# Softmax denominators from summed key blocks, with the sum made on GpSimd, in a fused macaron block on one Trainium2 core

## The chip, the cores and the metric

The kernel runs on one core of one Trainium2 chip. The metric is the device time of one execution in microseconds (us); lower is better. The engines are TensorE (PE, with its weight loads as PEld), VectorE (DVE), ScalarE (ACT), GpSimd (POOL) and SyncE (SP, which issues most of the DMAs here). Each works through its own queue in program order; semaphores order them among each other.

## The reference

For 16 batches of 512 tokens with 128 features, everything in fp32:

```python
x = x + 0.5 * ffn(layernorm(x))     # 128x128 weight rounded to int4 steps, bias, rank-16 LoRA
x = x + attention(layernorm(x))
x = x + 0.5 * ffn(layernorm(x))

# attention: 16 heads, head size 64, keys and values from a latent of 32 per token
q = einsum('bld,dhk->blhk', x, Wq);  latent = einsum('bld,dc->blc', x, Wkv_down)
k = einsum('blc,chk->blhk', latent, Wk_up);  v = einsum('blc,chk->blhk', latent, Wv_up)
p = softmax(causal(q @ k.T / 8))     # 512 x 512 per head
y = einsum('bhqk,bkhd->bqhd', p, v);  out = einsum('bqhd,hdo->bqo', y, Wout)
```

## The kernel before, in words

The key and value projections are folded into the query and output weights, so that scores and weighted sums are taken against the 32-wide latents. There are H = 16 heads in G = 4 groups of HG = 4, and four key blocks of P = 128 keys.

A *round* `t` handles several batches at once: attention of batch t (`attend`), the row maxima of batch t+1 (`top`), the first feed-forward, queries and keys of batch t+2 (`prep`, "front units") and projection and second feed-forward of batch t-1 (`end`, "tail units"). Rounds go from -2 to 16, so rounds 1 to 13 hold all four kinds of work. A round has 16 steps; step s = 4g + j is group g and key block j. By causality block j only matters for queries from 128j on, so a step has 512 - 128j query columns per head: 512, 384, 256, 128.

The order in a step is written out by hand for each engine:

- TensorE, `score(s, e)`: scores with keys on the partitions, up to 512 columns in one of two PSUM banks. One call fills a bank: one head in blocks 0 and 1, two heads (256 columns each) in block 2, four heads (128 each) in block 3, with one matmul per head. A bank may be overwritten when ACT has read it (`exp_done`, two units back).
- ACT, `exp(s, e)`: one exponential per bank, into `probs`, four buffers of [128, 4 heads, 512], one per step in turn. Each is free again when `pv_done` says that TensorE has finished with it.
- POOL: one `affine_select` per step zeroes the upper triangle of the diagonal 128x128 blocks of the four heads, and signals `p_ready`.
- TensorE, two steps later (`LAG` = 2), between its second and third score calls: `weigh_latents` multiplies the probabilities of step s-2 with the latents (four matmuls, one per head, each with 32 output partitions of one bank, `y_bank`); `weigh_ones` multiplies the same probabilities with ones, which adds up each query's denominator. `group_ones` puts the four groups' sums on different partitions, and `den_bank` accumulates over all 16 steps.
- Maximum units, 41 a round: one or two matmuls into one of three ring banks and a VectorE reduction each (`max_unit`). The table `A_AT` lists for each step where among the scores they stand (slots 0 to 5).
- ACT copies `y_bank` to `y_sb` after each group and `den_bank` to `den` in step 2 of the next round. VectorE inverts `den` (steps 2, 3) and spreads it over the heads with shuffles (steps 4, 5). POOL multiplies (`scale_y(0..3)`, four times 512 elements) to `y_norm`, in steps 5 and 6; TensorE's `project_out` in step 7 needs all four.
- POOL also does small chains for the layer norms (`scale_and_bias`, with a power of -0.5; `first_rstd` in step 14) and adds the bias in two places (`xb`, `x2b`). VectorE normalises the next-but-two batch in step 15 (line 898: four `tensor_scalar` of 128 columns, SBUF to SBUF), and TensorE's first front unit in step 0 transposes the result.

## Time and profile before

| | |
|---|---|
| median of 3 runs | 1002.56 us (999.51 to 1003.19) |
| the profiled execution's own time | 1000.99 us |
| its span in the profile | 999.3 us |
| a full round (from one copy of `den` to the next) | 56.1 us |
| the last round with attention | 40.4 us |
| TensorE / VectorE / ACT / GpSimd busy in the span | 94% / 68% / 54% / 36% |
| granted TensorE clock, mean | 0.974 |

Times are those of one profiled execution. A busy TensorE is not one at its peak: matmuls overlap, and their ends are modelled, so the distance from one start to the next tells what an instruction costs.

### The profile page before, as it was taken

Reading aid. Unit: us, or ns where it says so; the run is one execution under the profiler, and the core shown is the slowest. Engines: PE = TensorE matmul, PEld = TensorE weight load, DVE = VectorE, ACT = ScalarE, POOL = GpSimd, SP = SyncE. Lnnn points to the kernel's source line nnn. Section 1 sums busy time; section 2 is a strip of 40 time slices with the busy share of each in tenths; the row PEclk is TensorE's granted clock in tenths of the full one; section 3 lists DMA queues with packets and bytes.
Section 4 is the critical chain, followed back from the end, with each engine's and each line's share of the span. In section 5 each row is a group of like instructions: output and inputs, shape, how many; then the busy total and the mean of one; then the engine's idle time right before and its main releaser. Section 6 shows DMA issues by size and latency. Waiting matters only on the chain. (4 is left out here: it accounts for less than half of the span.)

```text
span 999.3 us, 20244 instructions
## 1 busy us (share of the span) xinstructions
PE 936.8 (94%) x7518; PEld 579.5 (58%) x7518; DVE 677.7 (68%) x1526; ACT 536.5 (54%) x1065; POOL 364.4 (36%) x551
## 2 busy tenths in 40 slices
PE   4678999999999999999999999999999999999873
PEld 3345556566565656566565666566565666555433
DVE  4468577778767677678767677678767677576311
ACT  3242655556655555556656555556656555545550
POOL 4101234353433424253433425253533525233333
PEclk9968999999999999999999999999999999999995
DMA  3436251433425141433425141433425241420000
GB/s 81 96 81 139 52 114 45 96 95 76 115 64 125 41 104 47 101 89 76 115 65 126 43 102 47 103 88 76 114 65 125 48 99 34 108 62 12 13 22 11
DMA packets 77538, 77.81 MB, mean 78 GB/s; under 512 B 9392, under 2 KB 51136, under 8 KB 77440
## 3 DMA queue, kind: packets, MB, share of 16 engines
q1 hardware_dynamic: 75296, 74.76, 31.7%
q10 hardware_dynamic: 2144, 1.75, 0.7%
q8 instruction: 60, 0.98, 0.4%
q14 instruction: 38, 0.31, 0.1%
HBM read 9.90 MB, written 8.39 MB: 18 GB/s over the span
## 5 line engine op out<-in xcount | busy, mean ns | idle before, releaser
L470 ACT ACTIVATE probs<-bank 128x512 f32<-128x512 f32 (+1 forms) x704 | 376.3, 559 | 309.9 <-PE bank L591 307.2
L421 POOL TENSOR_SCALAR_AFFINE_SELECT probs<-probs 128x512 f32<-128x512 f32 x256 | 162.8, 637 | 531.9 <-ACT probs L470 530.6
L848 DVE TENSOR_REDUCE maxima<-bank 128x1 f32<-128x512 f32 (+1 forms) x384 | 255.9, 681 | 124.6 <-PE bank L649 124.3
L591 PE MATMUL bank<-q_stack,keys 123*128 123x512 f32 (+3 forms) x1024 | 326.0, 384 | 4.8 <-ACT probs L470 4.5
L649 PE MATMUL bank<-keys,q_stack 122*128 122x512 f32 (+3 forms) x1024 | 256.4, 333 | 7.0 <-DMA q_stack<-q_low 2.8
L649 PEld LDWEIGHTS bank<-keys,q_stack 122*128 122x128 f32 x1024 | 177.4, 193 | 97.8 <-issue 46.2
L591 PEld LDWEIGHTS bank<-q_stack,keys 123*128 123x128 f32 x1024 | 167.8, 190 | 101.9 <-issue 52.0
L848 DVE TENSOR_REDUCE block_max<-bank 128x4 f32<-128x512 f32 x256 | 174.3, 681 | 34.3 <-PE bank L649 34.1
L605 PE MATMUL bank<-probs,lat 128*32 128x512 f32 (+3 forms) x2048 | 190.9, 444 | 1.0 <-ACT y_sb L477 0.6
L616 PE MATMUL bank<-probs,group_ones 128*32 128x512 f32 (+3 forms) x2048 | 185.2, 433 | 0.6 <-ACT den L519 0.5
L616 PEld LDWEIGHTS bank<-probs,group_ones 128*32 128x32 f32 x2048 | 63.9, 110 | 78.9 <-issue 53.8
L397 POOL TENSOR_TENSOR y_norm<-y_sb,y_norm 128x512 f32<-128x512 f32 x64 | 80.5, 1281 | 6.6 <-DVE y_norm L866 6.6
L674 PE MATMUL bank<-xn_t,w_query 128*128 128x512 f32 x128 | 71.4, 645 | 4.7 <-DVE q_low L914 2.9
L499 ACT ACTIVATE q_high<-bank 128x512 fp32r<-128x512 f32 x64 | 38.4, 600 | 65.0 <-PE bank L674 64.8
L698 PE MATMUL bank<-w_out,y_norm 128*128 128x128 f32 x512 | 62.6, 283 | 10.4 <-POOL y_norm L397 10.4
L605 PEld LDWEIGHTS bank<-probs,lat 128*32 128x32 f32 x2048 | 40.6, 108 | 53.7 <-issue 37.8
L698 PEld LDWEIGHTS bank<-w_out,y_norm 128*128 128x128 f32 x512 | 62.2, 199 | 11.9 <-issue 11.3
L861 DVE RECIPROCAL den_inv<-den 128x128 f32<-128x128 f32 x64 | 55.8, 916 | 12.6 <-ACT den L519 12.6
L880 DVE TENSOR_TENSOR x<-bank,x_back 128x512 f32<-128x512 f32 x16 | 11.1, 692 | 56.5 <-PE bank L698 56.5
L914 DVE TENSOR_TENSOR q_low<-bank,q_high 128x512 fp32r<-128x512 f32 x64 | 43.6, 681 | 6.9 <-ACT q_high L499 6.9
L866 DVE STREAM_SHUFFLE y_norm<-den_inv 128x512 f32<-128x512 f32 x64 | 46.0, 749 | 0.0
L477 ACT ACTIVATE y_sb<-bank 128x512 f32<-128x512 f32 x64 | 38.0, 593 | 4.7 <-POOL y_norm L397 2.8
(106 smaller groups left out, 632.4 us busy)
## 6 DMA issues: line engine op xcount, KB each, us to landing
q_stack<-q_high SPq DMA_DIRECT2D x256, 128.0 KB, 2.4
q_stack<-q_low SPq DMA_DIRECT2D x128, 128.0 KB, 2.5
out_dram<-x SPq DMA_DIRECT2D x32, 256.0 KB, 2.4
x_in<-in_L_attn_x_bld_dram SPq DMA_DIRECT2D x16, 256.0 KB, 3.3
x_back<-out_dram SPq DMA_DIRECT2D x16, 256.0 KB, 3.1
keys<-keys_staged SPq DMA_DIRECT2D x15, 192.0 KB, 2.5
keys<-keys_staged SPq DMA_DIRECT2D x30, 96.0 KB, 2.3
lat<-lat_staged SPq DMA_DIRECT2D x16, 64.0 KB, 1.9
```

Of the source, the lines that this page charges most:

```text
L397: nc.gpsimd.tensor_tensor(y_norm[:, g, :], y_sb[:, g, :], y_norm[:, g, :], ALU.mult).then_inc(y_normed, 1)
L421: nc.gpsimd.affine_select(out=diag, in_=diag, compare_op=ALU.is_ge, fill=0.0, base=0, pattern=[[0, HG], [1, n]], channel_multiplier=-1).th ...
L470: nc.scalar.activation(probs[s % BUFS][:, e:e + heads, 0:n], scores[u % 2][:, 0:heads * n].rearrange("p (e q) -> p e q", e=heads), ACT.Exp ...
L591: last = nc.tensor.matmul(scores[u % 2][:, i * n:(i + 1) * n], keys[par][:, PLAIN_BLOCK[j], :], q_stack[par][:, g * HG + e + i, j * P:L], ...
L605: last = nc.tensor.matmul(y_bank[e * LD:(e + 1) * LD, j * P:L], lat[(par + off) % 2][:, j, :], probs[s % BUFS][:, e, 0:L - P * j], start=( ...
L616: last = nc.tensor.matmul(den_bank[e * LD:(e + 1) * LD, j * P:L], group_ones[:, g, :], probs[s % BUFS][:, e, 0:L - P * j], start=(s == 0), ...
L649: last = nc.tensor.matmul(bank[:, col:col + n], q_stack[1 - par][0:KC, half * HALF + h, j * P:(j + 1) * P], keys[1 - par][0:KC, blocks, :] ...
L674: last = nc.tensor.matmul(bank[:], w, xn_t[:], start=True, stop=True)
L698: last = nc.tensor.matmul(aux[:, i * D:(i + 1) * D], y_norm[:, g, i * P:(i + 1) * P], w_out[:, g, :], start=(g == 0), stop=(g == G - 1))
L848: nc.vector.tensor_reduce(out, seg, AX.X, ALU.max).then_inc(a_free, 1)
L861: nc.vector.reciprocal(den_inv[:, part], den[:, part]).then_inc(den_made, 1)
L866: nc.vector.stream_shuffle(y_norm[:, g, :], den_inv[:], [g] * LD).then_inc(den_made, 1)
```

## The change

1. The denominators take fewer matmuls. GpSimd adds the probabilities of key blocks 1 and 2 onto those of block 0 (`add_probs`), in place, for the queries that they share (384 and 256 columns of each head). Each addition is made in two parts of two heads: 768 elements per partition twice and 512 twice in a group. `weigh_ones` is now called once per group, in step 4g+5, and takes block 0 with the sum, and block 3.
2. The additions stand in POOL's queue in steps 4g+2 and 4g+3, one part in front of the step's select and one behind. The first waits until the latents of step 4g are weighed, since it overwrites their input. The pieces that POOL has in the queue besides are moved: `scale_y` to steps 4, 5, 5, 6; `scale_and_bias` one step earlier, behind the select.
3. The probabilities' buffers change: two for block 0 (`first_probs`) and one each for blocks 1, 2, 3 (`later_probs`). `pv_done` is signalled after the latents; `added` and `den_done` are new.
4. `weigh_latents` moves behind the step's third score slot in steps with j = 3.
5. `score` issues one matmul over all heads that share a bank (2 x 256 or 4 x 128 columns) in place of one per head.
6. `A_AT` is another table; the number of units is the same.

```diff
-A_AT = [[], [0, 1, 1], [0, 2, 3], [], [2, 3, 3, 5], [0, 5], [1, 4], [2, 2], [0, 3, 3, 5], [0, 1, 4], [0, 2], [0, 1, 1, 4, 5], [0, 1, 2, 3], [0, 0, 1, 3], [1, 2], [4]]
+A_AT = [[], [1, 1, 2], [0, 2], [3, 5], [0, 2, 5], [0, 1, 1, 5], [0], [1], [3], [0, 1, 4, 5], [0, 1, 1, 2, 4], [4, 5, 5], [0, 2, 3], [0, 1, 4, 5], [0, 0, 2, 3], [5]]
...
+WEIGH = [[2], [2], [2], [2]]
+WEIGH_SLOT = [1, 1, 1, 3]
+WEIGH_ONES = [[], [2], [], []]
+PARTS = 2
+ADD_AT = [(1, 0, 2, 0), (1, 1, 2, 1), (2, 0, 3, 0), (2, 1, 3, 1)]
+SCALE_AT = [4, 5, 5, 6]
...
-BUFS = 4
+ADDED = [1, 2]
+DEN_PARTS = [j for j in range(TT) if j not in ADDED]
...
-        probs = [sb(f"probs{i}", [P, HG, L]) for i in range(BUFS)]
+        first_probs = [sb(f"first_probs{i}", [P, HG, L]) for i in range(2)]
+        later_probs = [sb(f"later_probs{j}", [P, HG, L - P * j]) for j in range(1, TT)]
...
+                def add_probs(off, g, j, part):
+
+                    turn = PARTS * (g * len(ADDED) + ADDED.index(j)) + part
+                    wait_batch(pool, pv_done, t, off, STEPS, g * TT + 1)
+                    wait_batch(pool, p_ready, t, off, STEPS, g * TT + j + 1)
+                    if j != ADDED[0]:
+                        wait_batch(pool, added, t, off, PARTS * G * len(ADDED), turn - PARTS + 1)
+                    heads = slice(part * HG // PARTS, (part + 1) * HG // PARTS)
+                    total = first_probs[g % 2][:, heads, j * P:L]
+                    nc.gpsimd.tensor_tensor(total, total, later_probs[j - 1][:, heads], ALU.add).then_inc(added, 1)
+
+                def adds(s, behind):
+
+                    for j, part, step, at in ADD_AT:
+                        if at == behind and (s - step) % TT == 0:
+                            if s >= step and attend:
+                                add_probs(0, (s - step) // TT, j, part)
+                            if s < step and end:
+                                add_probs(-1, (s - step + STEPS) // TT, j, part)
...
-                    if prep and s == FRONT_AT[1] + 2:
+                    for g in range(G):
+                        if end and s == SCALE_AT[g]:
+                            scale_y(g)
+                    adds(s, 0)
+                    if attend:
...
+                    if prep and s == FRONT_AT[1] + 1:
                         wait_batch(pool, f_normed, t, 1, 2, 2)
                         scale_and_bias(f_moments, 2, 2, f_mv[:, 1], f_var[:, 1], f_rstd[:, 1], f_shift,
                                        f_pool, 4, f_rstd_made)
...
+                    if end and s == TAIL_AT[0] + 1:
                         wait_batch(pool, t_normed, t, -2, 1, 1)
                         scale_and_bias(t_moments, 1, -1, t_mv, t_var[:], t_rstd[:], t_shift, t_pool, 3, t_rstd_made)
...
+                    adds(s, 1)
...
                     if e == 0:
-                        wait_batch(act, pv_done, t, 0, STEPS, s - BUFS + 1)
+                        wait_batch(act, pv_done, t, 0, STEPS, s - TT + 1)
+                        if j in ADDED:
+                            wait_batch(act, added, t, 0, PARTS * G * len(ADDED),
+                                       PARTS * ((g - 1) * len(ADDED) + ADDED.index(j) + 1))
+                        else:
+                            wait_batch(act, den_done, t, 0, G, g if j else g - 1)
...
-                    for i in range(heads):
-                        last = nc.tensor.matmul(scores[u % 2][:, i * n:(i + 1) * n], keys[par][:, PLAIN_BLOCK[j], :],
-                                                q_stack[par][:, g * HG + e + i, j * P:L], start=True, stop=True)
-                    last.then_inc(s_full, 1)
+                    first = g * HG + e
+                    nc.tensor.matmul(scores[u % 2][:, 0:heads * n], keys[par][:, PLAIN_BLOCK[j], :],
+                                     q_stack[par][:, first:first + heads, j * P:L], start=True, stop=True).then_inc(s_full, 1)
...
+                def weigh_ones(off, g):
+
+                    if g == 0:
                         wait_batch(pe, den_free, t, off, 1, 0)
-                    for e in range(HG):
...
-                    last.then_inc(pv_done, 1)
+                    for j in DEN_PARTS:
+                        if j == 0:
+                            wait_batch(pe, added, t, off, PARTS * G * len(ADDED), PARTS * (g + 1) * len(ADDED))
+                        else:
+                            wait_batch(pe, p_ready, t, off, STEPS, g * TT + j + 1)
+                        for e in range(HG):
+                            last = nc.tensor.matmul(den_bank[e * LD:(e + 1) * LD, j * P:L], group_ones[:, g, :],
+                                                    probs_of(g * TT + j)[:, e, 0:L - P * j],
+                                                    start=(g == 0 and j == 0),
+                                                    stop=(g == G - 1 and j == DEN_PARTS[-1]))
+                    last.then_inc(den_done, 1)
```

## Rows read from the trace of the kernel before

**Rows 1.** The page: span; busy us (share) and instructions by engine.

```profile
span 999.3 us, 20244 instructions
...
PE 936.8 (94%) x7518; PEld 579.5 (58%) x7518; DVE 677.7 (68%) x1526; ACT 536.5 (54%) x1065; POOL 364.4 (36%) x551
...
```

**Rows 2.** Waits: who waited for whom, us in total, times, longest.

```profile
...
POOL probs L421 <- ACT probs L470: 530.6, 176, 8.0
...
PEld bank L591 <- ACT probs L470: 46.3, 153, 0.9
...
```

**Rows 3.** Windows: length, busy us (instructions) by engine, granted clock, DMA.

```profile
...
372.70:428.80 56.10, 55.97 (x468) 34.75 (x464) 41.54 (x95) 32.47 (x68) 22.26 (x33) 1.00 0.36 86
...
877.40:928.80 51.40, 49.71 (x432) 29.52 (x424) 32.29 (x65) 27.35 (x56) 18.03 (x26) 1.00 0.12 29
928.80:969.20 40.40, 36.82 (x353) 19.43 (x346) 8.74 (x22) 22.55 (x46) 17.00 (x24) 1.00 0.05 14
969.20:979.20 10.00, 0.00 (x0) 0.00 (x0) 6.04 (x12) 0.60 (x2) 4.94 (x4) 0.60 0.00 0
...
```

**Rows 4.** Timeline, TensorE, a steady round: start us, us, what.

```profile
...
429.41 1.07 PE L616 MATMUL bank<-probs,group_ones 128*32 128x512 f32 x8
430.41 0.51 PE L649 MATMUL bank<-keys,q_stack 122*128 122x256 f32 x2
...
431.23 0.56 PE L591 MATMUL bank<-q_stack,keys 123*128 123x128 f32 x4
431.72 0.85 PE L605 MATMUL bank<-probs,lat 128*32 128x384 f32 x8
432.39 0.83 PE L616 MATMUL bank<-probs,group_ones 128*32 128x384 f32 x8
...
433.81 0.64 PE L605 MATMUL bank<-probs,lat 128*32 128x256 f32 x8
434.27 0.61 PE L616 MATMUL bank<-probs,group_ones 128*32 128x256 f32 x8
...
435.15 0.45 PE L591 MATMUL bank<-q_stack,keys 123*128 123x512 f32 x1
435.43 0.62 PE L649 MATMUL bank<-keys,q_stack 122*128 122x512 f32 x3
...
438.13 0.43 PE L605 MATMUL bank<-probs,lat 128*32 128x128 f32 x8
...
445.98 3.73 PE L698 MATMUL bank<-w_out,y_norm 128*128 128x128 f32 x32
...
454.50 0.43 PE L605 MATMUL bank<-probs,lat 128*32 128x128 f32 x8
...
473.04 1.04 PE L616 MATMUL bank<-probs,group_ones 128*32 128x512 f32 x8
...
481.93 0.43 PE L605 MATMUL bank<-probs,lat 128*32 128x128 f32 x8
...
```

**Rows 5.** Groups by form, POOL: busy us, mean ns of one, idle before.

```profile
...
L397 POOL TENSOR_TENSOR y_norm<-y_sb,y_norm 128x512 f32<-128x512 f32 x64 | 80.5, 1281 | 6.6 <-DVE y_norm L866 6.6
...
L385 POOL TENSOR_TENSOR t_shift<-t_shift,t_rstd 128x4 f32<-128x4 f32 x16 | 3.3, 204 | 1.3
...
```

**Rows 6.** Timeline of POOL in the same round.

```profile
...
432.57 0.23 POOL L380 TENSOR_SCALAR f_var<-f_mv 128x4 f32<-128x4 f32 x1
...
434.46 0.64 POOL L421 TENSOR_SCALAR_AFFINE_SELECT probs<-probs 128x512 f32<-128x512 f32 x1
...
438.47 2.51 POOL L397 TENSOR_TENSOR y_norm<-y_sb,y_norm 128x512 f32<-128x512 f32 x2
...
```

**Rows 7.** Timeline of POOL and DVE around line 898, twice.

```profile
...
44.45 1.26 POOL L425 TENSOR_TENSOR xb<-x_in,half_bias 128x512 f32<-128x512 f32 x1
44.52 2.05 DVE L898 TENSOR_SCALAR xn<-x_in,f_mv,f_rstd 128x128 f32<-128x128 f32 x4 [0.87 <-POOL f_rstd L391]
...
478.88 1.11 DVE L898 TENSOR_SCALAR xn<-x_in,f_mv,f_rstd 128x128 f32<-128x128 f32 x4
...
```

More of the change, by code:

```diff
@@ L213, in macaron_block @@
         pv_done = sem("pv_done")
-        y_full = sem("y_full")
+        added = sem("added")
+        den_done = sem("den_done")
         y_free = sem("y_free")
@@ L233, in wait_batch_alone, with probs_of @@
             eng.sem_inc(waits_passed, 1)
+        def probs_of(s):
+            return later_probs[s % TT - 1] if s % TT else first_probs[s // TT % 2]
         def stages(t):
@@ L474, in read_y @@
                 def read_y(off, g):
-                    wait_batch(act, y_full, t, off, G, g + 1)
+                    wait_batch(act, pv_done, t, off, STEPS, TT * (g + 1))
                     wait_batch(act, y_normed, t, off - 1, G, g + 1)
@@ L515, in one_round @@
                         normalise(xn3, x2, t_rstd, t_shift, range(TT // 2))
-                    if s == LAG and end:
-                        wait_batch(act, pv_done, t, -1, STEPS, STEPS)
+                    if s == DEN_READ and end:
+                        wait_batch(act, den_done, t, -1, G, G)
                         nc.scalar.activation(den[:], den_bank[:], ACT.Copy).then_inc(den_free, 1)
@@ L527, in one_round @@
                         exp(s, 2)
-                    if s == LAG - 1 and end:
+                    if s == Y_READ - 1 and end:
                         read_y(-1, G - 1)
-                    if s >= LAG and (s - LAG + 1) % TT == 0 and attend:
-                        read_y(0, (s - LAG) // TT)
+                    if s >= Y_READ and (s - Y_READ + 1) % TT == 0 and attend:
+                        read_y(0, (s - Y_READ) // TT)
                     if attend:
@@ L605, in weigh_latents @@
                         last = nc.tensor.matmul(y_bank[e * LD:(e + 1) * LD, j * P:L], lat[(par + off) % 2][:, j, :],
[L606 to L618 removed]
+                                         probs_of(s)[:, e, 0:L - P * j], start=(j == 0), stop=(j == TT - 1))
+                    last.then_inc(pv_done, 1)
+                def weigh_ones(off, g):
+                    if g == 0:
+                        wait_batch(pe, den_free, t, off, 1, 0)
+                    for j in DEN_PARTS:
[9 more added lines that the diff above has]
+                    last.then_inc(den_done, 1)
                 def max_unit(v):
@@ L716, in one_round, with weigh_steps @@
                     tiles = units_of(s) if top else []
+                    def weigh_steps(slot):
+                        for lag in WEIGH[s % TT] if slot == WEIGH_SLOT[s % TT] else []:
+                            off, back = (0, s - lag) if s >= lag else (-1, s - lag + STEPS)
+                            if attend if off == 0 else end:
+                                weigh_latents(off, back)
+                        for lag in WEIGH_ONES[s % TT] if slot == WEIGH_SLOT[s % TT] else []:
+                            off, back = (0, s - lag) if s >= lag else (-1, s - lag + STEPS)
+                            if attend if off == 0 else end:
+                                weigh_ones(off, back // TT)
                     def max_units(slot):
@@ L722, in max_units @@
                                 max_unit(v)
-                    off, back = (0, s - LAG) if s >= LAG else (-1, s - LAG + STEPS)
-                    weigh = attend if s >= LAG else end
                     if attend:
@@ L731, in one_round @@
                     max_units(1)
-                    if weigh:
-                        weigh_latents(off, back)
-                        weigh_ones(off, back)
+                    weigh_steps(1)
                     max_units(2)
```

38 lines of the change are left out of this document (14 added, 24 removed).

## The prediction

> **What bounds the kernel now.** I read the page first. The profiled execution has a span of 999.3 us and a time of 1000.99 us, and GpSimd (POOL) is busy for only 36% of it against VectorE's 68% [rows 1]. Busy time is a poor guide for TensorE, so I went to the waits next: POOL spends 530.6 us waiting for ScalarE's exponentials, while TensorE's weight loads wait for ScalarE for only 46.3 us in the whole run [rows 2]. The windows say the same of one round (one batch in steady state, cut at the copy of `den`, 56.1 us): TensorE 55.97 us busy at a granted clock of 1.00, DVE 41.5, ACT 32.5, POOL 22.3 [rows 3]. The order of matmuls on TensorE sets the pace in a full round. In the last round with attention (928.8 to 969.2) there are no maxima and no front units, and TensorE already has idle gaps: 36.8 us in 40.4 [rows 3].
>
> **What TensorE saves.** A busy matmul includes a drain that overlaps the next, so I price by distance from start to start [rows 4]. The ones matmuls of key block 1 (384 columns) begin 0.67 us after the latents of the same block, and those of block 2 (256 columns) cost 0.46 (434.27 to 433.81). Both go, in each of four head groups: 4 x (0.67 + 0.46) = 4.5 us a round. Those of block 0 (1.00 us, 429.41 to 430.41) and of block 3 stay; they are only moved, to step 4g+5. The first of these 1.00 includes about 0.1 of changing from narrow to wide weights, which stays behind the latents. In block 3 four score matmuls of 128 columns take 0.49 us (431.23 to 431.72); one of 512 columns takes 0.28 (435.15 to 435.43); so 0.21 a group. In block 2 two matmuls of 256 columns become one of 512, twice a group; the columns are the same, so between 0 and 0.12 each; I take the upper end, because there a weight load goes as well. That is 4 x (0.21 + 0.24) = 1.8. TensorE alone would need 6.3 us less a round, 49.8 in place of 56.1.
>
> **What GpSimd adds.** The trace has no add of 768 elements. The multiply of 512 elements takes 1.281 us, the one of 4 elements 0.204 [rows 5]; the line through both gives 2.12 ns an element and 1.82 us for 768. Back to back an instruction takes about 0.03 less than its duration (two y_norm in 2.51 us), and a select 0.64 [rows 6], so I use 1.79, 1.25 and 0.61. Below, an add of 768 can't be cheaper than one of 512, 1.25; above, in proportion, it is 1.5 x 1.281 = 1.92. One head group costs 2 x 1.79 + 2 x 1.25 = 6.1 us and the round 24.3 us, so POOL goes from 22.3 to 46.6 us in a round of 49.8. That average would still just fit. The order in its queue decides, since POOL works strictly in order and each of its waits holds all behind it.
>
> **The new loop.** The first add of group g waits for the latents of step 4g, which TensorE issues in step 4g+2. Then POOL does, one behind another: add 1.79, select 0.61, add 1.79, add 1.25, select 0.61, add 1.25 = 7.3 us. Only then may TensorE start the ones of the group (step 4g+5), and the select of block 3, 1.25 earlier, gates the latents in front of them. Behind that wait stand TensorE's own scores of step 4g+5, hence ACT's exponentials, the select of 4g+5 and the latents whose end starts the next group's adds. So it is a loop through both engines, not a free queue.
>
> *First group.* I count from the end of its latents (429.41). `scale_and_bias` now stands among the adds; its four links took 1.9 us (432.57 to the next select at 434.46) [rows 6]. So the sum is complete at 7.3 + 1.9 = 9.2. TensorE reached that place 8.7 us later (438.13) [rows 4]; it now saves 0.9 + 0.67 + 0.46 of ones, 0.4 of scores, and has two more maximum units in front (9 against 7 by the table `A_AT`, about 0.28 each), so it is there at 6.9 and waits 2.2 us. Then POOL owes scale_y(0), a select, scale_y(1), scale_y(2), a select and scale_y(3): 4 x 1.25 + 2 x 0.61 = 6.2, done at 15.4. `project_out` needs all four. Before, it started 16.6 us behind the latents (445.98) [rows 4]. TensorE could now be there at 13.4 (less 0.9 + 0.67 + 0.46 + 0.67 of ones, 0.5 of scores); it gets its input at 15.5. This stretch gives 1.1 us and not 3.2.
>
> *Rest of the round*, 56.1 - 16.6 = 39.5 us. TensorE saves the other 3.1 here. Second group: POOL is ready at 15.4 + 7.3 = 22.7; before, the step-9 latents came 8.5 us behind project_out (454.50) [rows 4], now 0.46 less and three maximum units fewer (0.84), so at 15.5 + 7.2 + 0.24 = 22.9: a tie. The third group has more room before it and x2b (1.25) in it: again within 0.3. Fourth group: 8.9 us before (473.04 to 481.93) [rows 4], less 0.9 + 0.67 + 0.46 + 0.2 = 6.7, plus 0.24, against 7.3: a wait of 0.4.
>
> *VectorE's normalisation*, line 898, lies in just this stretch. Alone, its four instructions take 1.11 us (478.88). Once, at 44.52, they were issued together with a GpSimd addition (44.45, 1.26 us) and took 2.05: they ended as late as if the first had sat out the addition [rows 7]. After the change they are issued while POOL is inside the fourth group's adds, in every round. TensorE's transposes (`front_unit(0)`) wait for the fourth of them. I take the row's 0.9 us as the price; it is never negative, and 1.3 is what two blocking instructions (an add and a select) would cost beyond their overlap. That takes in most of the fourth group's 0.4. The rule for this is in the Trainium skill, "SBUF — State Buffer", section "Who interferes with whom": VectorE's `tensor_scalar` in its fast mode and a GpSimd instruction hold one port pair exclusively, and the second to issue fully blocks. The trace agrees at 44.52. By that rule alone each of the four could be blocked anew; the rival below has its price.
>
> Waits in the rest of the round are thus 0.3 + 0.9 + 0.2 = 1.4, and with some 0.5 more of ACT (it has the same 32.5 us of work in a shorter round, and two score banks only) it gives 3.1 - 1.9 = 1.2. A full round gains 1.1 + 1.2 = 2.3 us, to about 53.8.
>
> **Sum.** Full rounds are t = 1 to 13: 13 x 2.3 = 30. Round 0 has no scale_y and no projection: about 3. Round 14 (877.4 to 928.8) has no front units, so fewer extras for POOL and less cover from TensorE: about 2. Round 15 (40.4 us) loses. There TensorE's part from the adds' end to the next first add is ones 1.2, two scores, a score and latents, about 3.1, so a group takes 7.3 + 3.1 = 10.4 at least; the chain is 13.5 (with scale_y) + 10.4 + 11.7 (with x2b) + 7.3 + 1.2 = 44.1, against 39.4 now: -4.7. All in all 30 + 3 + 2 - 5 = 30 us. Against the profiled run's 1001.0 that is 971; the median of the runs is 1.6 higher, so 972.
>
> At nothing: the longer reach of the probability buffers (exp of a later block waits for adds of the group before, finished two steps earlier; if POOL ran a whole step later this would come up). SP's queue and all DMAs are untouched, only `pv_done` is signalled earlier. scale_and_bias is ready 1.79 + 0.61 + 1.9 = 4.3 us behind the first latents, but ACT wants it after the first exponential of step 4, at about 2.5. So ACT waits 1.8 us there, with three exponentials queued behind it; TensorE's scores of step 5 follow at about 8.1 and its latents at 8.6, still in front of POOL's 9.2. POOL's adds are the cover; without them it would cost up to 8.6 - 6.9 = 1.7 us a round.
>
> **Rivals.**
> *GpSimd stays hidden.* If the adds cost 1.25 for 768 elements too, the round is 4.3 us shorter on POOL, the ties become slack, and TensorE bounds: up to 14 x 6 - 5 = 80 us less, 910 to 945. For it: 46.6 is below 49.8. Against: the first group alone holds 15.4 us of POOL in TensorE's 13.4. 17%.
> *VectorE is blocked all along.* If each of the four line-898 instructions waits out its own GpSimd instruction (2 adds, 2 selects, 3.7 us and its own 1.1, so 2.6 more than I count), the transposes are late by that much, 14 times: +36, 988 to 1008. For it: 44.52. Against: there three of four ran free, though only one addition was there. 14%, 9 of them faster by over 0.5%. By the skill's page just named this is what a chain of adds would do.
> *Slower: the adds are dearer.* Each microsecond of them lies fully in the loop. My round has 2.3 us to lose, so from 24.3 + 2.3 = 26.6 us of adds (1.66 us for the mean add where I have 1.52, 9% more) there is no gain; at 20% more (29.2 us a round, gaps at the waits in front of each included) it is 4.9 x 16 = 78 us on my 972, so this case spans 1008 to 1050. For it: scale_and_bias's small instructions take 1.9 us from first to last, much of it gaps at waits. Against: 1.28 us for 512 is stable over all 64. 13%.
> *No effect*, within 0.5% (5 us, what a measurement of this kernel can tell): ties all come out a little worse, 6%.
>
> **Numbers.** The forecast, 50%, has 955 to 988 as its own range (the add at 1.7 to 1.92, port price 0 to 1.3). Faster: 50 + 17 + 9 + 2 of the margin = 78%; same: 5 + 4 = 9%; slower 13%. The range leaves out about one in ten at each end: 935 to 1005.
>
> **What would show it.** The adds of 768 elements near 1.8 us, of 512 near 1.28; POOL's busy time near 750 us. A round between two copies of `den` near 53.8; the ones of step 5 starting right behind the last add (TensorE idle <- POOL), and project_out right behind scale_y(3). Line 898's first instructions above 1 us. Round 15 longer than 40.4. Wrong if TensorE shows no wait for POOL, if adds cost far from 1.8, or if TensorE's granted clock leaves 1.00 in its new gaps (it fell to 0.60 only in the 10 us without matmuls, behind 969.2 [rows 3]).

## The result, and the profile after

| | before | after |
|---|---|---|
| median, device us | 1002.88 (999.51 to 1004.22) | 1043.72 (1038.69 to 1045.78) |
| ratio, after to before | | 1.0405 [1.0359, 1.0451] |
| span of the profiled execution | 999.3 | 1044.0 |

The change makes the kernel 4% slower. The forecast was 972, and the range (935 to 1005) doesn't hold the time.

I read the page of the changed kernel first: span, busy time and instructions of each engine, and the granted TensorE clock in 40 slices.

```profile
span 1044.0 us, 18096 instructions
...
PE 904.0 (87%) x6174; PEld 545.9 (52%) x6174; DVE 714.9 (68%) x1526; ACT 534.4 (51%) x1065; POOL 745.7 (71%) x807
...
PEclk9868989999999999989998999999899999998875
...
```

POOL is busy for 745.7 us, as forecast (about 750), and TensorE runs 1344 matmuls fewer than in [rows 1]. What was not forecast is the clock line: between the start-up and the last round three slices are eights, where the page of the kernel before has only nines, and the mean granted clock is 0.926 against 0.974.

Next its windows (columns as in [rows 3]): a steady round, the first groups of another round up to `project_out`, the rest of that round, the 3.4 us behind its last gap, the one full round that has no normalisation in its step 15, and the last round with attention.

```profile
...
565.70:623.80 58.10, 53.50 (x384) 33.71 (x380) 44.17 (x95) 32.31 (x67) 45.95 (x49) 0.94 0.35 82
624.40:640.10 15.70, 13.77 (x99) 7.16 (x95) 14.79 (x33) 9.54 (x21) 15.26 (x17) 1.00 0.16 48
640.10:682.30 42.20, 39.07 (x286) 25.18 (x286) 29.49 (x62) 22.61 (x46) 30.74 (x32) 0.96 0.42 96
674.70:678.10 3.40, 3.16 (x21) 2.82 (x25) 1.25 (x4) 1.36 (x3) 1.25 (x2) 0.50 0.94 207
855.80:909.90 54.10, 51.80 (x374) 31.21 (x368) 38.92 (x82) 31.82 (x66) 43.37 (x46) 0.97 0.31 73
962.10:1014.10 52.00, 41.71 (x271) 16.81 (x263) 8.74 (x22) 22.67 (x47) 40.82 (x40) 0.80 0.04 11
...
```

The steady round takes 58.1 us against 56.1, with less TensorE work in it (53.5 against 55.97 [rows 3]). The stretch from 624.4 to 640.1 took 15.7 us where the prediction had 15.5. So the loss is in the rest of the round (42.2 us), and within it there is a stretch in which the granted clock is 0.50, the 1.2 GHz level. (The round shown first has two such stretches of 3.4 us, at 572.3 and 616.6; 6 of the 13 full rounds have the one of the first group too, but they are at most 0.9 us longer than the others.) The full round of 855.8 to 909.9, in which VectorE has no next batch to normalise, takes 54.1. It also lacks the statistics of that batch, so it is no clean measure of what the others would take.

The groups by form in the changed kernel (busy us, mean ns of one, idle before): the two sizes of addition, and VectorE's normalisation, which is line 952. Below it is the same group in the kernel before, line 898.

```profile
...
L417 POOL TENSOR_TENSOR first_probs<-first_probs,later_probs 128x768 f32<-128x768 f32 x128 | 233.5, 1825 | 32.9 <-PE bank L644 32.9
...
L417 POOL TENSOR_TENSOR first_probs<-first_probs,later_probs 128x512 f32<-128x512 f32 x128 | 164.2, 1283 | 0.0
...
L952 DVE TENSOR_SCALAR xn<-x_in,f_mv,f_rstd 128x128 f32<-128x128 f32 x60 | 52.2, 930 | 0.9 <-POOL f_rstd L406 0.9
...
```

```profile
...
L898 DVE TENSOR_SCALAR xn<-x_in,f_mv,f_rstd 128x128 f32<-128x128 f32 x60 | 17.7, 357 | 0.9 <-POOL f_rstd L391 0.9
...
```

The additions cost what the prediction said (1.82 and 1.28). The normalisation went from 357 ns an instruction to 930. The waits (who waited for whom, us in total, times, longest) say who pays:

```profile
...
PE bank L711 <- DVE xn L952: 42.2, 14, 3.1
...
ACT xn L522 <- POOL f_shift L400: 35.0, 16, 10.9
...
PEld bank L658 <- POOL first_probs L417: 5.9, 7, 1.1
...
PE bank L658 <- POOL first_probs L417: 4.8, 7, 0.9
...
```

TensorE waits for `xn` 14 times, 42.2 us in all. One of these waits, 1.9 us during the start-up (47.25), was there before the change; the 13 new ones are 3.1 us each. Its waits for the sums that GpSimd makes, the main step of the forecast, come to under 11 us in the whole run. In the 13 full rounds (157.9 to 909.9) they are next to nothing, and the same view has no wait of TensorE for `y_norm`:

```profile
...
PEld bank L658 <- POOL first_probs L417: 0.6, 2, 0.5
...
PE bank L658 <- POOL first_probs L417: 0.2, 1, 0.2
...
```

The timeline around one of the waits for `xn` (start, us, what; the time before an instruction and who ended it in brackets):

```profile
...
669.24 3.06 POOL L417 TENSOR_TENSOR first_probs<-first_probs,later_probs 128x768 f32<-128x768 f32 x2
...
671.02 3.77 DVE L952 TENSOR_SCALAR xn<-x_in,f_mv,f_rstd 128x128 f32<-128x128 f32 x4
...
671.54 0.27 PE L672 MATMUL bank<-identity,maxima 128*32 128x128 f32 x1
672.25 0.64 POOL L447 TENSOR_SCALAR_AFFINE_SELECT later_probs<-later_probs 128x512 f32<-128x512 f32 x1
...
672.85 1.27 POOL L417 TENSOR_TENSOR first_probs<-first_probs,later_probs 128x512 f32<-128x512 f32 x1
...
674.07 0.65 POOL L447 TENSOR_SCALAR_AFFINE_SELECT first_probs<-first_probs 128x512 f32<-128x512 f32 x1
...
674.67 1.28 POOL L459 TENSOR_TENSOR xb<-x_in,half_bias 128x512 f32<-128x512 f32 x1
...
674.94 1.09 PE L711 MATMUL bank<-identity,xn 128*128 128x128 f32 x4 [3.12 <-DVE xn L952]
...
```

VectorE's four instructions are issued at 671.02 and end at 674.79, 3.77 us later, where they took 1.11 [rows 7]. GpSimd's queue has addition, select, addition, select, `xb` in just these microseconds (the row at 669.24 holds two additions, and the second begins as VectorE issues). TensorE has done its last work at 671.8 and starts the transposes of `xn` at 674.94, having waited 3.12 us. They take 1.09, 0.63 where the clock is full, and the clock stays at 0.50 up to 678.1.

### The profile page after: what moved, and what is told of

Its sections match the earlier page's. It is cut to its first block and busy times, and to the rows that moved or that the text cites. A ratio compares the mean times of both kernels' runs of the same rounds, so it can differ in the third digit from the quotient of the medians.

```text
span 1044.0 us, 18096 instructions
## 1 busy us (share of the span) xinstructions
PE 904.0 (87%) x6174; PEld 545.9 (52%) x6174; DVE 714.9 (68%) x1526; ACT 534.4 (51%) x1065; POOL 745.7 (71%) x807
## 5 line engine op out<-in xcount | busy, mean ns | idle before, releaser
L417 POOL TENSOR_TENSOR first_probs<-first_probs,later_probs 128x768 f32<-128x768 f32 (+1 forms) x256 | 395.4, 1554 | 32.9 <-PE bank L644 32.9
L631 PE MATMUL bank<-q_stack,keys 123*128 123x512 f32 (+1 forms) x704 | 316.3, 479 | 20.1 <-ACT first_probs L510 18.0
L510 ACT ACTIVATE later_probs<-bank 128x384 f32<-128x384 f32 (+1 forms) x448 | 231.5, 536 | 192.8 <-PE bank L631 191.4
L447 POOL TENSOR_SCALAR_AFFINE_SELECT later_probs<-later_probs 128x512 f32<-128x512 f32 x192 | 122.9, 640 | 148.2 <-ACT later_probs L510 148.2
L510 ACT ACTIVATE first_probs<-bank 128x512 f32<-128x512 f32 x256 | 140.4, 593 | 105.5 <-PE bank L631 101.0
L631 PEld LDWEIGHTS bank<-q_stack,keys 123*128 123x128 f32 x704 | 132.6, 200 | 101.2 <-ACT first_probs L510 49.4
L644 PE MATMUL bank<-later_probs,lat 128*32 128x384 f32 (+2 forms) x1536 | 126.8, 404 | 6.7 <-POOL later_probs L447 6.7
L658 PE MATMUL bank<-first_probs,group_ones 128*32 128x512 f32 x512 | 74.9, 659 | 4.8 <-POOL first_probs L417 4.8
L644 PE MATMUL bank<-first_probs,lat 128*32 128x512 f32 x512 | 70.8, 626 | 0.1
L711 PE MATMUL bank<-identity,xn 128*128 128x128 f32 x128 | 29.2, 371 | 48.1 <-DVE xn L952 42.2
L644 PEld LDWEIGHTS bank<-later_probs,lat 128*32 128x32 f32 x1536 | 31.1, 111 | 64.7 <-issue 51.3
```

Source lines behind the costliest of these rows:

```text
L417: nc.gpsimd.tensor_tensor(total, total, later_probs[j - 1][:, heads], ALU.add).then_inc(added, 1)
L447: nc.gpsimd.affine_select(out=diag, in_=diag, compare_op=ALU.is_ge, fill=0.0, base=0, pattern=[[0, HG], [1, n]], channel_multiplier=-1).th ...
L510: nc.scalar.activation(probs_of(s)[:, e:e + heads, 0:n], scores[u % 2][:, 0:heads * n].rearrange("p (e q) -> p e q", e=heads), ACT.Exp).th ...
L631: nc.tensor.matmul(scores[u % 2][:, 0:heads * n], keys[par][:, PLAIN_BLOCK[j], :], q_stack[par][:, first:first + heads, j * P:L], start=Tr ...
L644: last = nc.tensor.matmul(y_bank[e * LD:(e + 1) * LD, j * P:L], lat[(par + off) % 2][:, j, :], probs_of(s)[:, e, 0:L - P * j], start=(j == ...
L658: last = nc.tensor.matmul(den_bank[e * LD:(e + 1) * LD, j * P:L], group_ones[:, g, :], probs_of(g * TT + j)[:, e, 0:L - P * j], start=(g = ...
```

## The experiments

Times are medians beside runs of the kernel before on the same chip (1000.8 to 1002.7). The code is shortened: `...` marks what is left out, and some comments are added. "Round" is the distance between two copies of `den` in steady state: 56.1 before, 58.1 after.

**1. The changed kernel with the normalisation two steps earlier**, and the statistics that feed it.

```diff
-if t + 3 < B and s == STEPS - 3:      # statistics
+if t + 3 < B and s == 11:
-if t + 3 < B and s == STEPS - 2:      # first_rstd (POOL)
+if t + 3 < B and s == 13:
-if t + 3 < B and s == STEPS - 1:      # normalise, before max_unit
+if t + 3 < B and s == 13:             # behind the third max_unit
```

> The changed kernel, with VectorE's statistics of the next-but-two batch in step 11 (was 13), GpSimd's first_rstd at the head of step 13 (was 14) and the four tensor_scalar of xn in step 13 (was 15), where GpSimd had 2.7 us of idle time. Nothing is left out. Theory A (the four tensor_scalar are held up by the adds, 3.77 us instead of 1.11, TensorE's transposes wait 3.1 us for them and the granted clock falls to half for 3.4 us behind the gap, worth 1.7 us): the group falls to about 1.1 to 1.5 us, TensorE's wait for xn is gone, a full round goes from 58.0 to about 53.5, the time to 970 to 985 us. Theory B (the loop of adds through GpSimd and TensorE sets the round, and the wait for xn only stands where another would): the wait turns into one for the adds, the round stays above 57 us, the time above 1025 us.

Measured: 1003.49, ratio 1.0015 [0.9998, 1.0033], 40 us less than the changed kernel. A steady round and the normalisation in its trace:

```profile
...
428.20:483.00 54.80, 51.98 (x384) 31.11 (x380) 42.53 (x95) 32.25 (x68) 46.08 (x49) 1.00 0.37 88
...
```

```profile
...
L980 DVE TENSOR_SCALAR xn<-x_in,f_mv,f_rstd 128x128 f32<-128x128 f32 x60 | 21.6, 424 | 1.0 <-POOL f_rstd L406 1.0
...
```

TensorE's wait for `xn` is gone, and the clock of this round is 1.00 (two of the 13 full rounds still have 3.4 us at 0.50). The round is 3.3 us shorter than in the changed kernel, not 4.5 as expected. Theory A is right on the place, but I had expected 970 to 985: the rest of the plan does not pay either. A second short VectorE instruction from SBUF to SBUF is slower beside the additions, a copy of 8 columns, 583 ns on the mean where it took 175 before:

```profile
...
L908 DVE COPY maxima<-block_max 128x8 f32<-128x8 f32 x32 | 18.7, 583 | 0.0
...
```

In this run TensorE waits for it 3.0 us in all.

**2. The changed kernel with six filler matmuls** (identity, 512 columns, into the bank that is overwritten next) in front of the wait, so that TensorE doesn't stand idle.

```diff
+if u == 0 and t >= 0:
+    for _ in range(6):
+        nc.tensor.matmul(bank[:], identity[:], w_out[:].rearrange("p g o -> p (g o)"), start=True, stop=True)
 if u in (0, 2):
     wait_batch(pe, f_normed, t, 2, 2, 1 + u // 2)
```

> The changed kernel, with six matmuls of 512 columns (constant weights, into the bank that the transposes then overwrite) in front of TensorE's wait for xn in step 0 of every round from 0 on, 2.75 us of work in a gap of 3.1. They add nothing to the result. Theory A (the fall of the granted clock behind the gap costs time of its own): the clock stays at 1.00 around it, the transposes take 0.38 us again in place of 0.7, and the round loses 1.2 to 1.7 us, the time 1015 to 1025 us. Theory B (after the gap TensorE waits for GpSimd anyway, so that the slow stretch is hidden): same time, 1040 to 1047 us.

Measured: 1051.57, ratio 1.0497 [1.0474, 1.0521]. The six took 5.31 us and ended 2.1 us after `xn` was there, so the run mixes a gain and a loss. It says nothing by itself; number 5 repeats it with three.

**3. The changed kernel without any addition**: all four blocks' ones weighed directly behind the latents, everything else (table, buffers, merged scores, order) as changed.

```diff
 def add_probs(off, g, j, part):
+    if direct(t + off, g):            # here: always
+        return
 ...
 weigh_latents(off, back)
+weigh_ones_directly(off, back)       # four matmuls per block, as before
```

> The changed kernel without its additions: the ones matmuls take every key block again, right behind the latents of the same step; one score matmul per bank, the new table, buffers and positions stay. Nothing is left out. Theory A (the additions cost all of the loss, the rest of the change gains): full rounds of 54.3 to 55 us, the time 975 to 988 us. Theory B (the new table, the buffers or the wide score matmul cost as well): rounds of 56 us or more, 1000 us or more.

Measured: 1012.36, ratio 1.0106 [1.0083, 1.013]. Windows of a steady round and of the last one:

```profile
...
436.00:492.80 56.80, 55.86 (x448) 33.06 (x444) 41.77 (x95) 32.11 (x67) 22.07 (x33) 1.00 0.36 85
943.20:982.50 39.30, 36.23 (x335) 17.18 (x327) 8.74 (x22) 22.53 (x47) 17.10 (x24) 1.00 0.05 15
...
```

The last round is short again (39.3 against 52.0). But the steady round is longer than before the change, 56.8 at full clock, although no addition is left and the scores are merged. Theory B is right here: something besides the additions costs time.

**4. The kernel before with additions that nobody reads**, four a group, at the places where the change puts them; sizes, engine and count as in the change.

```diff
+def dead_add(n):
+    ...                               # waits for the addition before it
+    nc.gpsimd.tensor_tensor(scrap[:, 0:n], wq_in[:, 0:n], wq_in[:, 1024 - n:1024], ALU.add).then_inc(scrapped, 1)
+if attend and s % TT >= 2: dead_add(768 if s % TT == 2 else 512)   # before the select
+if attend and s % TT >= 2: dead_add(768 if s % TT == 2 else 512)   # and behind it
```

> The kernel before, with GpSimd additions of the same sizes at the same places in its queue (768, 768, 512, 512 elements per group, in steps 4g+2 and 4g+3, one ahead and one behind the select), from constants into a scratch tile that nobody reads. Nobody waits for them but GpSimd's own queue. Theory A (GpSimd's additions hold up VectorE's tensor_scalar of xn): this group goes from 1.1 to about 3.8 us, TensorE waits for it, clock falls, rounds of 58.5 to 61 us, the time 1040 to 1080 us, though no ones matmul waits. Theory B (only the dependence of the ones and of project_out on the additions costs): xn and the round as before, at most the projection late by 2 us, 1003 to 1030 us.

Measured: 1111.18, ratio 1.1085 [1.1056, 1.1114]. Groups by form, then the timeline around one normalisation:

```profile
...
L404 POOL TENSOR_TENSOR scrap<-wq_in 128x768 f32<-128x768 f32 x128 | 233.4, 1824 | 0.0
...
L404 POOL TENSOR_TENSOR scrap<-wq_in 128x512 f32<-128x512 f32 x128 | 163.6, 1278 | 2.7
...
L910 DVE TENSOR_SCALAR xn<-x_in,f_mv,f_rstd 128x128 f32<-128x128 f32 x60 | 52.4, 932 | 0.9 <-POOL f_rstd L393 0.9
...
```

```profile
...
590.72 3.78 DVE L910 TENSOR_SCALAR xn<-x_in,f_mv,f_rstd 128x128 f32<-128x128 f32 x4
590.73 0.64 POOL L431 TENSOR_SCALAR_AFFINE_SELECT probs<-probs 128x512 f32<-128x512 f32 x1
...
591.33 1.27 POOL L404 TENSOR_TENSOR scrap<-wq_in 128x512 f32<-128x512 f32 x1
...
592.54 0.64 POOL L431 TENSOR_SCALAR_AFFINE_SELECT probs<-probs 128x512 f32<-128x512 f32 x1
...
593.14 1.27 POOL L437 TENSOR_TENSOR xb<-x_in,half_bias 128x512 f32<-128x512 f32 x1
...
594.64 1.09 PE L679 MATMUL bank<-identity,xn 128*128 128x128 f32 x4 [3.29 <-DVE xn L910]
...
```

Nothing waits for these additions but POOL's own next instruction. Still the four `tensor_scalar` take 3.78 us, and the transposes come 3.29 us late. So the blocking is no matter of data or of the sum's place: it is GpSimd's being busy at that moment. The price, about 110 us, is larger than theory A said. TensorE has lost no work here, and rounds such as the one from 731.7 have a clock of 0.92; how the excess divides between the two was not tried.

**5. Number 2 with three fillers.**

```diff
-    for _ in range(6):
+    for _ in range(3):
```

> As the run with six filling matmuls, with three (2.6 us in place of 5.3, so that they end before xn is ready). The six ran 2.1 us past xn and cost the round only 0.1 us net, with the granted clock at 1.00. Theory A (the half clock behind the gap costs about 2 us of its own): TensorE's idle time before the transposes is 0.5 us or less, the clock stays at 1.00 behind it, rounds of 56 to 56.6 us, the time 1015 to 1022 us. Theory B (hidden by waits for GpSimd): rounds as in the changed kernel, 58.0, 1038 us or more.

Measured: 1023.29, ratio 1.0215 [1.0186, 1.0243]. Timeline, then windows of a round and of the 3.4 us behind the gap:

```profile
...
541.90 3.77 DVE L955 TENSOR_SCALAR xn<-x_in,f_mv,f_rstd 128x128 f32<-128x128 f32 x4
...
542.60 2.74 PE L710 MATMUL bank<-w_out,identity 128*128 128x512 f32 x6
...
545.73 0.42 PEld L714 LDWEIGHTS bank<-identity,xn 128*128 128x128 f32 x4 [1.23 <-DVE xn L955]
...
```

```profile
...
494.80:551.10 56.30, 54.01 (x390) 32.27 (x386) 44.13 (x95) 32.06 (x67) 45.87 (x49) 1.00 0.35 84
545.70:549.10 3.40, 3.37 (x36) 2.34 (x37) 1.46 (x3) 1.36 (x3) 1.14 (x1) 1.00 0.94 202
...
```

VectorE's group still takes 3.77 us and TensorE still does nothing useful for 3.1. Only the clock is now 1.00 where it was 0.50, and the round is 56.3 and not 58.1. So the half clock alone is worth about 20 us (1.7 a round); the wait itself is still in this time.

**6. Number 3 with the table `A_AT` of the kernel before.**

```diff
-A_AT = [[], [1, 1, 2], [0, 2], [3, 5], ...]
+A_AT = [[], [0, 1, 1], [0, 2, 3], [], ...]
```

> The changed kernel without its additions (the ones take every key block), and with the old table A_AT of the maximum units. In the run with the new table the units took TensorE 13.1 us a round from start to start, in the kernel before 11.5, and 0.7 us of idle time stood before them, mostly for VectorE's reductions. Theory A (the new table crowds the units so that the ring of three banks waits for VectorE): the units fall back to 11.5, the round to 55.2, the time to 985 to 990 us. Theory B (the buffers or the later slot of the latents cost, not the table): units at 13, rounds of 56.5 or more, 1008 us or more.

Measured: 992.65, ratio 0.9913 [0.9889, 0.9936]; a round:

```profile
...
426.20:481.70 55.50, 55.25 (x448) 32.86 (x444) 41.37 (x95) 32.22 (x67) 22.12 (x33) 1.00 0.38 90
...
```

20 us less than number 3: without additions the new table costs 1.3 us a round. The maximum units took 11.6 us of a round's starts here and 13.1 in number 3 (worked out from the starts in the timeline). So the something of number 3 is the table.

**7. The kernel before with the merged score matmuls alone.**

```diff
-for i in range(heads):
-    last = nc.tensor.matmul(scores[u % 2][:, i * n:(i + 1) * n], ..., q_stack[par][:, g * HG + e + i, j * P:L], ...)
+nc.tensor.matmul(scores[u % 2][:, 0:heads * n], ..., q_stack[par][:, first:first + heads, j * P:L], ...)
```

> The kernel before with one part of the change alone: one score matmul over the heads that share a bank. Theory A (worth 0.8 us of start-to-start time a round, as in the run without additions, where scores fell from 15.2 to 14.3): rounds of 55.2 to 55.4, the time 988 to 992 us. Theory B (scores are paced by ACT's exponentials, so the gain turns into waits): 55.9 to 56.1, 1000 us or more.

Measured: 992.02, ratio 0.991 [0.9886, 0.9934], rounds of 55.5. This part of the change is worth 9 us. It equals number 6, so without additions the new buffers, the later latents in steps with j = 3, the moved `scale_y` and `scale_and_bias` and the new semaphores cost nothing in sum.

**8. Number 4 with the normalisation moved as in number 1.**

> The kernel before with the scratch additions that nobody reads, and VectorE's normalisation moved to step 13 (statistics 11, first_rstd 13) as in the first run. Theory A (VectorE's four tensor_scalar behind GpSimd's additions are the larger part of the loss of 8 us a round that the scratch additions brought): TensorE's wait of 3.3 us for xn and the half clock behind it are gone, rounds from 64.1 to 58 to 60 us, the time 1030 to 1050 us. Theory B (the loss comes from selects late behind additions, and latents waiting for them): rounds above 62 us, 1080 us or more.

Measured: 1053.03, ratio 1.0511 [1.0491, 1.0531]: 58 us less than number 4, by the same edit. The normalisation is at 358 ns again, the clock at 1.00 in most of the steady rounds, and a round at 58.8 on the mean. What is left, some 51 us over the kernel before, comes with the additions in POOL's queue while TensorE's work is undiminished; through which waits was not separated.

**9. Number 1 with the old table.**

> The changed kernel with VectorE's normalisation early (as in the first run) and the old table of the maximum units. Theory A (the table's 1.1 to 1.5 us a round come off here as they did without the additions): rounds from 55.0 to 53.5 to 53.9, the time 980 to 988 us. Theory B (with the additions GpSimd's loop sets the round, and the units only fill its waits): rounds of 54.7 or more, 998 us or more.

Measured: 1027.71, ratio 1.0229 [1.0193, 1.0265]. I had expected a gain from the table, as in number 6, and it is 24 us slower. Two neighbouring rounds:

```profile
...
498.50:555.00 56.50, 51.59 (x384) 30.96 (x380) 41.30 (x95) 32.15 (x67) 46.11 (x49) 1.00 0.35 83
441.50:498.50 57.00, 53.14 (x384) 31.64 (x380) 41.37 (x95) 32.30 (x68) 46.16 (x49) 0.97 0.33 79
...
```

The table's worth changes sign: with all the additions the new one is better by some 2 us a round (means of 54.9 and 57.1), without them it is worse by 1.3. The normalisation is at 357 ns here, so it isn't the cause. The clock is a part only: the second of the two rounds has 0.97, but the first, at 1.00, is still 1.7 us longer than the round of number 1 at 1.00.

**10. Number 9 with the last round's ones weighed directly** (`direct(t, g)` is `t == B - 1`).

> As the run before, and in round 15, the last with attention, the ones take every key block and nothing is added. Theory A (there TensorE has too little other work to cover GpSimd's additions, and the round takes 50.9 us with them against 40.5 without): 9 to 11 us less than the run before. Theory B (its length comes from ACT or the half clock at the end): 0 to 4 us less.

Measured: 1017.24, ratio 1.0142 [1.0113, 1.017]. The last round takes 39.7 us and not 50.0: the additions cost 10.3 us there.

**11. Number 10, with group 0 direct in every round as well** (`g == 0 or t == B - 1`).

> As the run before, and in every round the first head group too takes its ones from every key block, without additions. TensorE has 1.1 us more of ones a round, GpSimd 6.1 us less, in the stretch in which scale_and_bias and the four scale_y stand behind its additions. Theory A (this stretch is set by GpSimd: 15.7 us from the first latents to the projection where TensorE needs 13.4): it falls to about 14.5, the exponentials' wait for scale_and_bias (35 us in all) goes back to about 20, and the round falls by 1 to 2 us more, 945 to 965 us. Theory B (TensorE is the bound): the round grows by 1.1, 15 us more than the run before.

Measured: 996.06, ratio 0.993 [0.9915, 0.9945]; rounds of 55.3. 21 us less: in the group whose additions stand in POOL's queue just ahead of `scale_y`, they cost more than they save. The gain is at the upper end of the 1 to 2 us a round expected over number 10; the time is above the 945 to 965 because those were counted from a time for number 10 that had itself not come true. ScalarE's wait for `f_shift` fell as well, to 25.0 us in all.

**12. Number 11 with the new table.**

> The run with the first group and the last round without additions and the early normalisation, but with the new table. With the additions the old table was 2.1 us a round dearer than the new (57.1 against 55.0), without them 1.4 us cheaper. Theory A (the new table spreads the units where GpSimd's additions leave TensorE waiting; three of four groups still have them): rounds of 53.2 to 54.5, the time 970 to 983 us. Theory B (with only three groups the balance lies between, or VectorE's crowding costs as without additions): rounds of 55 or more, 990 us or more.

Measured: 980.02, ratio 0.9773 [0.9748, 0.9797]; rounds of 54.1. It is 16 us faster than number 11, so the new table is still the better one with the additions in three groups of four.

**13. The changed kernel with one edit: the fourth group without additions** (`g == G - 1`). The normalisation stays in step 15.

> The changed kernel with one edit: the fourth group of every round takes its ones from every key block and adds nothing. VectorE's normalisation stays in step 15. TensorE has 1.1 us more of ones a round. Theory A (it is the fourth group's additions, and only they, that block the normalisation): its four instructions take 1.1 to 1.6 us, TensorE's wait for xn is below 0.5, the clock stays at 1.00, rounds from 58.0 to 54 to 55.3 us, the time 990 to 1005 us. Theory B (selects and other additions block it as well, or the loop through GpSimd is what counts): it stays above 2.5 us, rounds above 57, 1030 us or more.

Measured: 991.69, ratio 0.9876 [0.984, 0.9913]. A round, and the normalisation:

```profile
...
480.60:535.10 54.50, 52.54 (x400) 31.69 (x396) 41.43 (x95) 32.04 (x67) 40.05 (x45) 1.00 0.37 86
...
```

```profile
...
L987 DVE TENSOR_SCALAR xn<-x_in,f_mv,f_rstd 128x128 f32<-128x128 f32 x60 | 17.6, 357 | 0.9 <-POOL f_rstd L417 0.9
...
```

With no addition in POOL's queue during step 15 the four instructions are back at 357 ns, the clock at 1.00 and the kernel 52 us faster, though TensorE does more ones.

**14. Additions only in groups 1 and 2, and none in the last round** (`g in (0, G - 1) or t == B - 1`), all else as changed.

> The changed kernel with additions in the second and third group only, and none in the last round; normalisation in step 15 as it was. Theory A (the additions pay where GpSimd has room and block nothing: in two groups of four): rounds of 53.5 to 54.8, the time 972 to 988 us. Theory B (what they save there, 1.1 us of ones a group, is lost to waits in the same groups): rounds near 56.8 less 0 to 1, 1000 to 1010 us, as without additions and with the same table.

Measured: 973.34, ratio 0.9711 [0.9685, 0.9738]. A steady round and the last one:

```profile
...
474.80:528.70 53.90, 53.54 (x416) 32.10 (x412) 41.41 (x95) 32.06 (x67) 34.11 (x41) 1.00 0.36 84
902.80:943.40 40.60, 37.67 (x335) 17.40 (x327) 8.73 (x22) 22.40 (x46) 17.13 (x24) 0.96 0.05 15
...
```

This is the fastest version: 2.9% faster than the kernel before and 70 us faster than the changed one.

## Why the prediction was wrong

**The step that failed is the price of VectorE's normalisation.** The prediction saw that the group would fall beside the fourth group's additions and took 0.9 us, from the one early collision [rows 7], with 1.3 as the upper end. The group measured 3.77 - 1.11 = 2.7 us more, and TensorE's wait 3.1. The row at 44.52 was a poor guide: there GpSimd had one addition and then nothing, here it has five instructions end to end, and the four of VectorE take as long as an addition, a select, an addition and a select of GpSimd's: the last one ends just as the fifth has begun. The second rival ("blocked all along", 2.6 us a round more) had this mechanism; the Trainium skill's rule ("SBUF — State Buffer", "Who interferes with whom": the second to issue fully blocks) agrees with 3.77, 3.78 and 3.77 us in three kernels. It had 14%, and its time (988 to 1008) was still too low, because of the next points.

**A term was missing: the clock after the gap.** The prediction named it only as something that would make it wrong, and its sum has nothing for it. TensorE's idle 3.1 us is followed by about 3.4 us at the granted clock 0.50. Number 5 removes this alone: 1.7 us a round, 20 us in all. The prediction also read the kernel before wrongly: it said that the clock had left 1.00 only behind 969.2. The trace has three more such stretches in the start-up. One of them follows a gap of 2.86 us, and was a row from which this term could have been priced (timeline, then window):

```profile
...
73.93 2.07 PE L674 MATMUL bank<-xn_t,w_query 128*128 128x512 f32 x2 [2.86 <-DVE q_low L914]
...
```

```profile
...
73.50:76.90 3.40, 2.97 (x7) 1.81 (x7) 2.00 (x4) 0.60 (x1) 0.00 (x0) 0.51 0.44 93
...
```

With both put in, 53.8 + (3.1 - 0.9) + 1.7 = 57.7, against 58.1 measured. Number 13 agrees: 58.1 - 3.1 - 1.7 plus 1.1 for the fourth group's ones is 54.4, and it measured 54.5. Number 1 does not: without the wait and the half clock it should take 53.3, and it takes 54.8 to 54.9. So the 57.7 comes this near in part by luck, and what stands behind the other 1.5 us was not separated.

**Nor do the two together make up the whole miss.** With the normalisation moved away (number 1) the kernel is still 31 us above the forecast of 972. By its copies of `den` it is 9 us late at the first, its full rounds take 14 us more than forecast, round 14 (52.3 us) takes 3 more and the last one (50.9) takes 6. The 13 full rounds as one window:

```profile
...
154.20:867.40 713.20, 677.14 (x4936) 405.63 (x4928) 549.25 (x1210) 418.85 (x859) 596.11 (x622) 1.00 0.37 86
...
```

**The waits for GpSimd came out elsewhere than forecast.** The prediction had TensorE wait 2.2 us for the sum of each first group, and called itself wrong if TensorE showed no wait for POOL. In the full rounds it shows 0.8 us in all. The chain in GpSimd's queue is as forecast: in the stretch from 624.4 the sum is complete 9.4 us and the last `y_norm` 15.5 us behind the latents (forecast 9.2 and 15.4). But TensorE loses its time earlier. ScalarE waits for `f_shift`, which `scale_and_bias` now makes behind an addition, and TensorE then waits for ScalarE to free a score bank:

```profile
...
629.04 0.88 ACT L522 ACTIVATE xn<-x,f_shift,f_rstd 128x128 f32<-128x128 f32 x2 [1.28 <-POOL f_shift L400]
...
```

```profile
...
630.45 0.50 PE L631 MATMUL bank<-q_stack,keys 123*128 123x512 f32 x1 [1.18 <-ACT first_probs L510]
...
```

This is the wait that the prediction put at nothing, since GpSimd's chain would cover it. Both routes end within 0.2 us of each other (ones at 633.94, the sum complete at 633.79), so the trace does not tell which one sets the 15.7 us.

**Where the 45 us of the spans went.** From the start to the first of these copies of `den` (148.5 before, 157.9 after) +9.4, where two of the 14 gaps lie (47.25, which is not new, and 149.75); 13 full rounds +23 (752.0 against 728.9); round 14 +0.8; the last round +11.6. The forecast had -3, -30, -2 and +4.7.

**The last round was mis-sized.** Its direction was right; it took 52.0 us and not 45. Number 10 shows that the additions are the cause (-10.3 without them). The prediction's chain priced no clock there, and it was 0.80; whether the clock accounts for all of the missing 7 us was not tried.

**The table was counted as neutral**, by its number of units. It isn't: 20 us worse without additions (3 against 6), 24 better with all of them (1 against 9). Why its sign turns was not settled; the clock is only a part of it (number 9).

**The scores' saving** was forecast at 1.8 us a round; number 7 gives 0.6, 9 us in all. By the starts in the timeline they went from 15.2 to 14.5 us a round. Why they kept the rest wasn't separated.

**Right:** the additions' durations (1.825 and 1.283 us against 1.82 and 1.28), POOL's busy time, and the length of the first stretch (15.7 against 15.5), with GpSimd's chain in it. The rival "the additions are dearer", which ended on the slower side, is refuted: the slowdown came with additions at their forecast price. That 1043.7 lies in its 1008 to 1050 is chance. ScalarE's wait for `f_shift` rose to 35.0 us in all; in the kernel before it was:

```profile
...
ACT xn L482 <- POOL f_shift L385: 21.6, 16, 10.5
...
```

It is 35.3 in number 13 too, so it isn't what separates that run from the changed kernel. In number 14 it is back at 20.0, and there the round is 0.6 us shorter than in number 13 although TensorE does more ones; but the first group's additions are gone there as well, so its own price stays open.

**What the parts come to.** Merged scores -9 (7). New table +20 (3 against 6). Additions in all groups +31 on that (1043.7 against 1012.4), of which the blocked normalisation and its clock are more than all: with it moved away the additions gain 9 (1003.5 against 1012.4). They gain more where POOL and VectorE are free: 973.3 with two groups of four.

## What to carry to other kernels

Before work goes to GpSimd, look for VectorE's short `tensor_scalar` instructions and copies that read and write SBUF and would then stand beside it, and who waits for them: price a group of them as if each waits out a GpSimd instruction of its own, not one for them all. If TensorE waits behind it, add the time at the lower clock after the gap, and look in the trace of before for a gap of that size to price it from. And an offload needn't be all or nothing: where a queue or a port is crowded, leave those pieces where they were; an order tuned for one load has to be tuned again for the other.

## What the runs showed of the hardware

- Four `tensor_scalar` of 128 columns took 1.11 us alone and 3.77 beside a chain of GpSimd instructions, whether these had anything to do with the data (changed kernel) or not (number 4). Additions that nobody reads made a kernel about 110 us slower.
- A copy of 8 columns, SBUF to SBUF, took 175 ns on the mean before and 583 in number 1. Other VectorE instructions did not slow down, although GpSimd was busy twice as long: the reciprocals from `den` to `den_inv` 916 ns before and 918 after, the shuffles 749 and 742, the statistics of `x_in` 278 and 279. A `tensor_scalar` that reads PSUM (`max_t`) took its usual 0.27 us at 674.71, beside `xb` on GpSimd.
- A TensorE gap of 3.1 us was followed by 3.4 us at a granted clock of 0.50, and in the kernel before one of 2.86 us by 3.4 us at 0.51; with the gap of 3.1 us filled by useless matmuls up to its last 0.40 us, the clock was 1.00.
- GpSimd's additions did not pay for the collisions: the one at 672.85, which holds up the normalisation, took 1.27 us, and all 128 of its size 1.283 on the mean.
- A filler matmul of 512 columns with operands in plain fp32 took 0.89 us (5.31 us for six, in number 2), three times the 0.28 of a score matmul of 512 columns [rows 4], whose operands the program writes as fp32r.
